# One core, cross-attention and two attention layers with a feed-forward: the rows of score maxima sent by three transfers instead of one

## What is computed

```python
qh = split(q @ wq + bq)
kh = split(k @ wk + bk)
vh = split(v @ wv + bv)
logits = jnp.einsum('bhqd,bhkd->bhqk', qh, kh) / jnp.sqrt(jnp.float32(depth))
logits = logits + mask * -1000000000.0
attn = jax.nn.softmax(logits, axis=-1)
out = jnp.einsum('bhqk,bhkd->bhqd', attn, vh)
out = out.transpose(0, 2, 1, 3).reshape(Bq, Sq, D)
return out @ wo + bo
...
out1 = _layernorm(x + attn1, ln1_g, ln1_b)
out2 = _layernorm(out1 + attn2, ln2_g, ln2_b)
ffn = jax.nn.relu(out2 @ ffn_w1 + ffn_b1) @ ffn_w2 + ffn_b2
return _layernorm(out2 + ffn, ln3_g, ln3_b)
```

## Time and profile before

| | us |
|---|---|
| median of 3 runs | 4418.93 |
| lowest and highest | 4416.27 and 4428.58 |
| the profiled execution, its own time | 4420.31 |
| its span, first to last instruction | 4418.5 |

### The profile page before, as it was taken

One profiled execution on the slowest core, in us unless ns is written; L12 is line 12 of the kernel. 1 busy time (PEld: TensorE's weight loads), 2 busy tenths in 40 slices (PEclk: granted clock), 3 DMA queues, 4 the chain that ended last, 5 costly groups with the idle time before them and its releaser, 6 DMA issues. The chain is left out here.

```text
span 4418.5 us, 129316 instructions
## 1 busy us (share of the span) xinstructions
PE 4103.6 (93%) x46152; PEld 3371.3 (76%) x46152; DVE 3534.5 (80%) x13895; ACT 3138.8 (71%) x6279; POOL 2887.1 (65%) x4576
## 2 busy tenths in 40 slices
PE   7999999999999979999999987999999997999999
PEld 6777777777777757777777766888878876999998
DVE  7999999999999969999999985777777774555555
ACT  5777777777777758888888875777777775454443
POOL 4777777777777747777777765676676762444444
PEclk8999999999999989999999998999999999999999
DMA  5444444444444456666666746778777872222221
GB/s 137 123 126 122 124 126 121 126 122 125 126 121 125 115 107 165 163 167 172 163 177 159 174 129 159 192 194 200 192 193 198 192 174 89 72 72 72 72 72 53
DMA packets 813639, 608.75 MB, mean 138 GB/s; under 512 B 61592, under 2 KB 751304, under 8 KB 813000
## 3 DMA queue, kind: packets, MB, share of 16 engines
q1 hardware_dynamic: 800952, 594.90, 51.1%
q10 hardware_dynamic: 12048, 5.58, 0.6%
HBM read 175.66 MB, written 117.54 MB: 66 GB/s over the span
## 5 line engine op out<-in xcount | busy, mean ns | idle before, releaser
L1048 ACT ACTIVATE mha_probs<-bank 128x512 f32<-128x512 f32 x1024 | 611.1, 600 | 282.3 <-DVE bank L1222 147.2
L1207 DVE CUSTOM_DVE_ANT_0 l_junk<-bank,mask 128x256 bf16<-128x256 f32 x2048 | 776.2, 417 | 35.2 <-PE bank L878 19.8
L1048 ACT ACTIVATE l_probs<-bank 128x512 f32<-128x512 f32 x1024 | 600.2, 593 | 160.3 <-DVE bank L1222 149.5
L1222 DVE TENSOR_TENSOR bank<-bank,mask0t 128x512 f32<-128x512 f32 x832 | 573.0, 689 | 6.2 <-PE bank L910 3.9
L1207 DVE CUSTOM_DVE_ANT_0 mha_junk<-bank,mask 128x128 bf16<-128x128 f32 x2048 | 462.0, 284 | 33.9 <-PE bank L878 33.7
L878 PE MATMUL bank<-mha_stack 96*128 96x128 bf16 (+1 forms) x4096 | 356.5, 221 | 77.0 <-DVE mha_max_parts L1207 47.8
L1630 ACT ACTIVATE ffn_hidden<-ffn_h,ffn_b_s 128x512 f32<-128x512 f32 x256 | 176.3, 689 | 353.5 <-PE ffn_h L1576 342.5
L1357 POOL TENSOR_TENSOR mha_yproj<-mha_yproj,mha_parts 128x512 f32<-128x512 f32 x252 | 292.9, 1162 | 190.7 <-ACT mha_parts L1021 187.2
L910 PE MATMUL bank<-mha_stack 99*128 99x128 bf16 (+1 forms) x4096 | 397.3, 221 | 18.1 <-DMA mha_stack<-mha_max_rows 12.8
L910 PE MATMUL bank<-l_stack 99*128 99x128 bf16 x4096 | 402.5, 220 | 7.5 <-ACT l_probs L1048 3.4
L878 PE MATMUL bank<-l_stack 96*128 96x256 bf16 x2048 | 375.2, 275 | 31.0 <-DVE l_max_parts L1207 25.4
(11 more groups left out here) (198 smaller groups left out, 11353.8 us busy)
## 6 DMA issues: line engine op xcount, KB each, us to landing
mha_stack<-mha_parts SPq DMA_DIRECT2D x1530, 128.0 KB, 3.5
l_stack<-l_parts SPq DMA_DIRECT2D x1024, 64.0 KB
l_stack<-l_parts SPq DMA_DIRECT2D x256, 128.0 KB
rows_o<-mha_resid SPq DMA_DIRECT2D x64, 512.0 KB, 2.7
cols_o<-mha_y_t SPq DMA_DIRECT2D x64, 512.0 KB, 3.5
l_x_pad<-in_x SPq DMA_DIRECT2D x64, 256.0 KB, 3.4
l_c_pad<-in_ctx SPq DMA_DIRECT2D x64, 256.0 KB, 3.1
l_resid<-in_x_t SPq DMA_DIRECT2D x64, 256.0 KB, 3.2
```

The costliest lines, as they stand in the source:

```text
L1048: nc.scalar.activation(probs[:, i % RING, :], tbank[i % 2][:, :], ACT.Exp).then_inc(att_exp, 1)
L1207: ins = nc.vector.tensor_tensor_reduce(out=junk[:, i % 2, cols], in0=sbank[i % 2][:, cols], in1=mask, scale=1.0, scalar=LOWEST, op0=ALU.ad ...
L1222: nc.vector.tensor_tensor(bank_, bank_, mask.unsqueeze(1).to_broadcast([P, 4, P]), ALU.add).then_inc(att_masked, 1)
```

## The change

In the second and third stage the single transfer of 48 rows becomes three transfers of 16 rows, one for each part, all issued by ScalarE one right behind the other, on the same semaphore; the counts that are waited for are multiplied by three. The first stage stays as it is.

```diff
--- before.py
+++ after.py
@@ -446,6 +446,7 @@
     STACKED = SCORED + 3
     ONES = (2 if phase == 2 else 1) * 16
     RING = 8
+    MAX_SENDS = 1 if conv else 3
 
     def own(n, shape, dt=F32):
         return scope.enter_context(nc.sbuf_tensor(f"{name}_{n}", shape, dt))
@@ -892,7 +893,7 @@
         def attend_step(u, i):
             j, q, kt = ATT[i]
             if i % 8 == 0:
-                pe.wait_ge(max_in[i // 8], 16 * (u.u + 1))
+                pe.wait_ge(max_in[i // 8], 16 * MAX_SENDS * (u.u + 1))
                 if u.number() in (0, 1) and i == 0:
                     pe.wait_ge(ones_in[u.par], ONES)
             wait(pe, att_exp, CHUNKS * u.u + i - 1)
@@ -1030,13 +1031,16 @@
 
         def max_rows_out(u, half, bank_):
             if half == 1:
-                act.wait_ge(max_in[0], 16 * (u.u + 1))
+                act.wait_ge(max_in[0], 16 * MAX_SENDS * (u.u + 1))
             else:
-                wait(act, max_in[1], 16 * u.u)
+                wait(act, max_in[1], 16 * MAX_SENDS * u.u)
             nc.scalar.activation(max_rows[:, :], bank_[0:3 * H, 0:P].bitcast(BF16), ACT.Copy).then_inc(work_out, 1)
             act.wait_ge(work_out, work_count(u, "max", half))
-            act.dma_start(stack[SCORED:STACKED, u.par, side_of((0,)), 2 * half * P:2 * (half + 1) * P], max_rows[:, :]
-                          ).then_inc(max_in[half], 16)
+            tokens = slice(2 * half * P, 2 * (half + 1) * P)
+            for part in range(MAX_SENDS):
+                act.dma_start(stack[SCORED + 3 * part // MAX_SENDS:SCORED + 3 * (part + 1) // MAX_SENDS, u.par, side_of((0,)), tokens],
+                              max_rows[3 * H * part // MAX_SENDS:3 * H * (part + 1) // MAX_SENDS, :]
+                              ).then_inc(max_in[half], 16)
 
         def exp_step(u, i):
             if i % 4 == 0:
```

## The result

| | before | after |
|---|---|---|
| median of 4 runs, us | 4419.95 | 4535.79 |
| lowest and highest | 4416.27, 4428.58 | 4531.69, 4536.42 |
| span of the profiled execution, us | 4418.5 | 4533.7 |

The ratio is 1.0259, with a 95% interval of 1.0246 to 1.0272. First the page of after: its span, and the queue of the transfers in question (packets, MB, share).

The account below looks back on a forecast made before the run. ScalarE's chain behind the issue, not the landing, was taken to bind at the second stage's L957. Losses of 29 us (second stage), 16 (clock) and 32 (third) make 77 on 4418.93: 4496, called 4495, range 4460 to 4530.

Parts of the forecast that it names:

- The issue: Each 16-row issue by ScalarE takes 0.60 us, so ScalarE is held x = 1.15 us longer per half of a unit.
- A: Rival, not slower: a part's issue costs 0.43 us, like a tiny load; 4429 us; chance 0.20.
- C: Rival: each part's issue is as long as today's, 0.73 us; 4558 us; chance 0.10.
- The landing: Rows' arrival: a part lands 3.3 us after its issue, the last at 4.6 us, 0.35 beyond the slack.
- D: Rival: rows are not spread, each part lands 4.1 us after its issue, the last at 5.4; 4520 us; chance 0.08.
- Second stage, first half: ScalarE's L1059 slips 0.67 us, so TensorE's L957 starts late: 0.58 us lost a unit, covering the late landing's 0.35.
- Second stage, second half: L1053's result reaches TensorE's L935 late: 0.30 us beyond 0.85 of cover, plus 0.05 for late landings, per unit.
- The clock: Second stage: longer TensorE idling lowers the granted clock in a third of units, 10 × 1.6 = 16 us.
- Third stage, first half: L1059 feeds VectorE's L1182, which TensorE's L952 needs: cover 0.47 us, so 0.68 us lost a unit.
- Third stage, second half: Exponential late for L910, 0.2 us, and the chain L1021, L1357, L1394 to VectorE's L1244: together 0.4 us a unit.
- B, faster by the spread: Rival: sixteen engines instead of three bring the rows so early that TensorE's waits go; 4400 us; chance 0.04.
- What bounds the kernel now: Second stage, at L957: ScalarE's chain (issue, L1092, two exponentials, L1059) binds; the landing has slack to about 4.25 us.

Follow-up runs that it names:

- second_first_half: Kernel before, with three transfers only for the first half of a unit, only in the second stage: 4461.81 us, ratio 1.0095.
- three_sends_warm: Kernel after, plus 16 unread TensorE products of 128 columns ahead of the wait for the rows at the start of second-stage units: 4519.05 us, 1.0222.
- third_only: Kernel before, with three transfers in the third stage alone and one in the second: 4472.30 us, ratio 1.0118.
- before_deferred: Kernel before, its one transfer issued behind ScalarE's next activation in the first half of a unit: 4420.46 us, ratio 1.0000.
- two_sends: Kernel before, with two transfers (one part, then two parts) instead of one in the second and third stage: 4435.16 us, ratio 1.0033.
- third_spaced: Kernel before, with three transfers in the third stage alone, the second and third issued behind the exponentials of the next two slots: 4438.34 us, 1.0038.
- before_warm: Kernel before, plus 16 unread TensorE products ahead of the wait for the rows at the start of second-stage units: 4417.79 us, ratio 0.9995.

## Why the prediction was right in direction and short in size

Its sum was 77 us, and 116 were measured. By its steps:

- **The issue.** 0.60 us for a part, x = 1.15. Measured 0.61 (0.51 for the first of three), x = 1.1 by the idle time behind it (1.93 - 0.82). This held, and with it fell A (an issue of 0.43 us) and C (0.73).
- **The landing.** A fill with its sixteen engines was the model, 3.3 us for a part; measured 2.9. The old transfer landed 3.9 us after its issue by the median, not 4.1. That the parts are spread shows in the packets: queue 10 has 12048 before and 17808 after, 5760 more, which is 45 for each of 128 halves; 51 + 45 = 96 = 3 × (16 + 16). So D fell. The last part lands 4.3 us after the first issue in the first half of a second-stage unit and 4.7 in the second (medians), as the 4.6 forecast. What I left out is the spread: one in ten comes 5.1 and 5.8 us after the first issue, or later.
- **Second stage, first half.** 0.58 us a unit. In second_first_half the 12 units that kept their clock take 32.41 against 31.90 us: 0.51. The term held for these units; all 26 take 33.34, 1.37 us more, and the difference is the clock, below. Of its two causes, which delay the same product, I had named ScalarE as the later. In the trace after both occur: in each of the 26 units L911 waits for the rows, 0.14 to 1.69 us, 11 times over 1 us, and in 13 L958 then waits for L1063. In the other 13 L958 waits 0.08 us at most: there the rows are the later. So the tail of the landing, which I had not counted, matters here.
- **Second stage, second half.** 0.35 us a unit, 11 us; the difference of two experiments is 30. With the clock this is the term that was mis-sized most in the second stage. The landing is not what was missing in it: between 1700 and 2550 us, after, 3 of the 25 second-half landings are waited for, 0.4 to 0.7 us, 1.8 us in all. L936 waits for `heads_out` in 12 units, 4.0 us in all (0.15 a unit, where I had 0.30) and, with the products of three_sends_warm, in 17, 12.8 us. The lengths say that the 30 us have two parts. Units that keep the clock go from 32.41 in second_first_half to 33.02 in after (12 and 5 units), and those that lose it from 14 of 26 to 21. What makes the first part stays open: the waits seen do not add up to it.
- **The clock.** 10 falls of 1.6 us in 31 units, 16 us. The pair with the products gives 17 us, but the agreement is luck: 21 of 26 units fall, not a third, and the lengths of units with and without a fall give up to 1.15 us a unit, 36 us. I had no row for the number of falls. Already second_first_half has 14 in 26.
- **Third stage, first half.** 0.68 us; measured 1.11 (33.5 us in the run that has only this). Here the step failed, not just a size. I followed the issue to L1059, L1182 and L952 and read 0.47 us of cover there. But L910, which follows at 3122.03 on TensorE in the kernel before, needs the first of the two exponentials right behind the issue, and in the units of the stage after it waits for it (28 times in the stretch shown above). L952 does not appear among the waits.

```profile
3121.18 1.09 ACT L1048 ACTIVATE mha_probs<-bank 128x512 f32<-128x512 f32 x2 [0.81 <-ACT mha_max_rows L1036]
```

```profile
3122.03 0.39 PE L910 MATMUL bank<-mha_stack 102*128 102x128 bf16 x4
```

  The consumer that comes first set the cover here, and not the longest chain.
- **Third stage, second half.** 0.4 us a unit, 12 us; measured 18.5 us, or 0.6 us a unit by this difference and 0.33 to 0.45 by the unit lengths (31.88 in after and 32.00 in third_only, against 31.55). About the size forecast, but by another path: L936 waits for `heads_out` in 12 of the units, 9.4 us, and I had named L910 and the chain over L1357 and L1394 to L1244. TensorE's wait at the end of that chain (L963, L964 after) is 18.1 us in 30 before and after.
- **B, faster by the spread.** Refuted: a part lands sooner than the one transfer did (2.9 us against 3.9), and the rows still come later, 4.3 and 4.7 us, since the last part is issued 1.2 us behind the first.
- **What bounds the kernel now.** I wrote that ScalarE's chain from the issue is what binds at L957. Too strong: before_deferred takes the issue out of that chain, and nothing changes, because VectorE's mask ahead of the exponential is late as well. My own number for this, the 0.48 us that L1059 can lose, fits two_sends, where 0.5 us of hold cost the stage 0.05 us a unit.

Sum of the measured terms: 68 us in the second stage, of which the clock is between 17 and 36 and the rest direct, and 1.44 × 30 = 43 in the third: 111 us, where I had 29 + 16 and 32. The direction and the mechanism, ScalarE standing still behind its issues, were right. The sum was short by the third stage's first consumer, by the second half of the second stage and by the falls of the clock.

The Trainium skill's rule on how many engines a transfer uses ("DMA: Bandwidth & Descriptors", section "Why a DMA increments its semaphore by 16 and not by 1") is borne out here: by it each part has 16 engines, and the trace shows 16 + 16 packets for each. That the last of three parts lands later than the one transfer did follows from the times of the issues, and these are read from the trace.

## What to carry to other kernels

Before a transfer is cut into more, spread pieces, count what the issuing engine stands still for each (here 0.5 to 0.6 us each), and look at the very next instruction of that engine and at who needs its result; two holds of 0.5 us in a unit were nearly free (0.05 and 0.37 us), two of 1.1 us cost 1.4 to 2.2 us. A landing is to be set against its need by its late tail too, and not by its median alone (here 4.3 us, with one in ten past 5.1). Where an issue must not hold an engine, put it behind an activation whose result it need not wait for, if the landing has time to spare.

## What the runs showed of the hardware that I had not expected

- An issue by ScalarE runs beside an activation ahead of it if it doesn't wait for it (third_spaced: 0.57 us of issue under 0.60 us of exponential).
- An issue's length is not set by its shape alone: 0.51 us for the first of three parts and 0.61 for the next; the transfer of 48 rows takes 0.73 us alone and 0.79 in the kernel with the two others behind it; single issues take up to 1.95 us. In the trace after, 12 of 384 took over 0.9 us, and 11 of them ran beside an issue of SyncE that took over 0.9 us too (of the 372 others, 42 did). Why was not tried.
- Sixteen products ahead of the first-half wait kept the clock at its upper level in all 26 units, where 21 had lost it, at no cost where there was next to nothing to keep (before_warm, 0.9995). What was left of that wait was at most 1.04 us. A wait of 2.4 us in a second half of the same run, without such products ahead of it, did not lower the clock either.
